# Output weights' squares moved from ScalarE to GpSimd, and the first norm's last step moved to ScalarE one set behind

## What is computed

```python
def _rfs(xw, ab, AB, gs):
    dot_products = jnp.einsum('...d,rd->...r', xw, ab[:, None] * gs)
    correction = (0.5 * jnp.sum(xw * xw, axis=-1))[..., None] * (ab * ab)
    return 1.0 / math.sqrt(NUM_RFS) * AB * jnp.exp(dot_products - correction)
weights = _rfs(input_weights, ab, AB, proj_matrix)
feats = _rfs(x, ab, AB, proj_matrix)
attn = jnp.einsum('bsr,or->bso', feats, weights)
x = _layernorm(x + attn)
gate, up = jnp.einsum('bsd,hd->bsh', x, wg), jnp.einsum('bsd,hd->bsh', x, wu)
x = _layernorm(x + jnp.einsum('bsh,dh->bsd', silu(gate) * up, wd))
```

## Time and profile before

| | |
|---|---|
| median of 3 runs | 609.4 us (609.28 to 609.42) |
| the profiled execution's own time | 610.9 us |
| its span on the slowest core (core 6) | 609.3 us; core 0 609.1, the 8 cores 605.9 to 609.3 us |
| TensorE busy | 590.8 us, 97% of the span |
| VectorE busy | 421.9 us, 69% |
| GpSimd busy | 381.9 us, 63% |
| ScalarE busy | 202.2 us, 33% |
| chain that ended last | TensorE 94%, transfers 3%, issue 1%, VectorE 1% |

### The profile page before, as it was taken

One profiled execution on the slowest core, in us unless ns is written; L12 is line 12 of the kernel. 1 busy time (PEld: TensorE's weight loads), 2 busy tenths in 40 slices (PEclk: granted clock), 3 DMA queues, 4 the chain that ended last, 5 costly groups with the idle time before them and its releaser, 6 DMA issues.

```text
span 609.3 us, 9120 instructions; the slowest of 8 cores (605.9 to 609.3 us)
## 1 busy us (share of the span) xinstructions
PE 590.8 (97%) x2649; PEld 266.1 (44%) x2703; DVE 421.9 (69%) x689; ACT 202.2 (33%) x375; POOL 381.9 (63%) x341
## 2 busy tenths in 40 slices
PE   5999999999999999999999999999999999999995
PEld 1444444444444444444444444444444444444442
DVE  2468323477788777777777777777777678876775
ACT  1234834447853322332232223222320015300243
POOL 9100899400093288999999999999516495604950
PEclk7988999999999999999999999999999999999999
DMA  8999471599930110422422413324424749983433
GB/s 143 155 169 235 154 234 34 169 279 324 232 85 2 69 40 32 164 93 73 165 86 80 165 47 118 116 84 158 146 104 126 254 147 306 318 266 136 175 138 140
DMA packets 45106, 90.79 MB, mean 149 GB/s; under 512 B 19328, under 2 KB 26496, under 8 KB 41728
## 3 DMA queue, kind: packets, MB, share of 16 engines
q1 hardware_dynamic: 36752, 59.52, 31.0%
q0 software_dynamic: 8160, 30.41, 19.3%
q10 hardware_dynamic: 144, 0.26, 0.1%
HBM read 60.82 MB, written 23.59 MB: 139 GB/s over the span
## 4 chain that ended last, share of the span: by engine, by line
PE 94%; DMA 3%; issue 1%; DVE 1%; POOL 0%; ACT 0%; DVEq 0%; ACTq 0%; POOLq 0%
PE P L597 47%; PE P L886 24%; PE P L321 9%; PE P L484 9%; PE P L366 5%; DMA proj<-projT 3%; PE P L399 1%; POOL xf L80 0%; POOL proj L80 0%; PE P L288 0%; PE P L290 0%; ACT junk L781 0%; DVE zh L829 0%; DVE wbuf L652 0%; DVE ebuf L616 0%
## 5 line engine op out<-in xcount | busy, mean ns | idle before, releaser
L597 PE MATMUL P<-x1t,ring 128*128 128x512 bf16 x753 | 180.1, 379 | 1.2 <-DVE ebuf L616 0.4
L210 POOL TENSOR_TENSOR ring<-ring 128x512 bf16<-128x512 bf16 x120 | 135.3, 1160 | 13.1 <-DMA ring<-wgu 9.6
L597 PE MATMUL P<-xsum,ring 128*128 128x512 bf16 x564 | 138.7, 379 | 0.6
L597 PEld LDWEIGHTS P<-x1t,ring 128*128 128x128 bf16 x768 | 75.0, 98 | 91.5 <-issue 1.6
L210 POOL TENSOR_TENSOR stage<-stage 128x512 bf16<-128x512 bf16 x60 | 68.1, 1170 | 46.1 <-DMA stage<-wd 44.2
L597 PEld LDWEIGHTS P<-xsum,ring 128*128 128x128 bf16 x576 | 56.4, 98 | 68.0 <-issue 0.4
L886 PE MATMUL P<-tbuf,hact 128*128 128x512 bf16 x376 | 83.3, 379 | 0.4
L321 PE MATMUL P<-xf,proj 128*128 128x512 bf16 x250 | 63.3, 413 | 6.0 <-ACT lnst L180 5.5
L886 PE MATMUL P<-tbuf,sbuf 128*128 128x512 bf16 x282 | 62.5, 379 | 0.3
L612 ACT ACTIVATE ebuf<-P 128x512 f32<-128x512 f32 x48 | 28.2, 588 | 101.4 <-PE P L597 101.4
L632 ACT ACTIVATE hact<-P 128x512 bf16<-128x512 f32 x48 | 28.5, 597 | 91.7 <-PE P L597 68.2
(11 more groups left out here) (94 smaller groups left out, 683.9 us busy)
## 6 DMA issues: line engine op xcount, KB each, us to landing
tbuf<-t_hbm SPq DMA_DIRECT2D x14, 1536.0 KB, 8.6
ring<-wgu POOLq DMA_DIRECT2D x12, 1024.0 KB, 5.3
xtok_sb<-xtok SPq DMA_DIRECT2D x16, 512.0 KB, 5.5
t_hbm<-stage SPq DMA_DIRECT2D x8, 896.0 KB, 4.4
stage<-wd POOLq DMA_DIRECT2D x12, 512.0 KB, 3.6
x_hbm<-x1k SPq DMA_DIRECT2D x16, 256.0 KB, 3.8
xres<-x_hbm SPq DMA_DIRECT2D x16, 256.0 KB, 6.5
out<-zd SPq DMA_DIRECT2D x8, 512.0 KB, 6.2
```

Source lines behind the costliest of these rows:

```text
L210: out[o] = (p.mark(eng, lambda e: e.tensor_tensor(d, a, b, op), *toks, *behind),)
L597: fn = lambda e, dk=dk, lhsT=lhsT, rhs=rhs: e.matmul(bank(b), lhsT, rhs, start=(start and dk == 0), stop=(stop and dk == 3), skip_group_ch ...
```

## The change

The squares of `norm_w` become GpSimd `tensor_tensor` multiplications. The place in the file is the same, but on GpSimd's queue they come behind the loads and ahead of all weight sums. All sets but the last have `apply` on ScalarE, with the shift as a 128x1 VectorE `tensor_tensor`, and the `apply` of a set is written behind the `root` of the next.

```diff
@@ norm_w
-        t_sq["w", k] = p.mark("scalar", lambda e: e.activation(sqw[:, a:b], iw[:, a:b], AF.Square), ld_iw[k])
+        t_sq["w", k] = p.mark("gpsimd", lambda e: e.tensor_tensor(
+            sqw[:, a:b], iw[:, a:b], iw[:, a:b], OP.mult), ld_iw[k])
@@
-    ON_ACT = range(7, NM - 1)
+    ON_ACT = range(NM - 1)
@@ apply
-                t_s = p.mark("scalar", lambda e: e.activation(shift, negm, AF.Copy, scale=rstd), t_r[0])
+                t_s = p.mark("vector", lambda e: e.tensor_tensor(shift, negm, rstd, OP.mult), t_r[0])
@@
         step = attn(i)
-        if 0 < i <= ON_ACT[0]:
-            last_norm[1]()
         if i < NM - 1:
             step[0]()
-        if i in ON_ACT:
-            step[1]()
+        if i > 0:
+            last_norm[1]()
```

## The result

The changed kernel takes **621.3 us** (median of 4 runs, 620.5 to 621.6) against 609.4 on the same chip: ratio 1.019, 95% interval 1.0178 to 1.0203, 11.9 us slower. The forecast was 624.0 in a range of 613 to 627. Its profiled execution took 620.5 us with a span of 619.0 on the slowest core, again core 6.

A forecast was written before the change was run, and what follows sets the result against it. TensorE, busy 97% of the span, was taken as the bound. For core 6, 11.0 + 1.7 + 1.25 + 0.6 = 14.6 us on the median 609.4 gave 624.0 us, range 613 to 627.

The forecast's parts named there:

- Turns of whole instructions: VectorE's five norm_x(3) instructions alternate with GpSimd's squares, each waiting for a whole instruction; they end at 73.5, not 56.7.
- The delay of 11.0: TensorE waits at feat_unit(3, 0) for banks whose evictions end at 76.7 but are wanted at 65.7: 11.0 us.
- The clock, 1.7: Work lost to a lower granted clock behind TensorE's long wait for banks: 1.7 us, bounds 0 and 3.4.
- Part 1: Squares leave ScalarE: core 0 loses its 2.0 us sbc wait and 1.7 us behind it; core 6 gains nothing.
- The seam, 1.25 + 0.6: At the first gate_up units: copy 1.25 us later behind set 14's shift, plus 0.6 for VectorE sums meeting GpSimd's.
- Part 3: apply on ScalarE, one set behind: nothing on TensorE's path, 10 us of matmuls ahead, except at the gate_up seam.
- A: Rival: VectorE's five norm_x(3) instructions are not held, or only by the first square; 610.7 us, chance 0.09.
- B: Rival: squares much faster than the sums, or only some of VectorE's five held; 613 to 619.5 us, chance 0.09.
- C: Rival, not slower: ScalarE's relief in w_unit(0) decides; 609.0 us, chance 0.05.

The follow-up runs named there:

- experiment 2: Kernel before with only the squares moved to GpSimd, in pieces of 1024 or 512 columns: 612.5 us (1.0055) and 611.7 us (1.003).
- norm_only: The changed kernel without the squares' move: squares stay on ScalarE, only the norm is changed; 611.75 us, ratio 1.0036.
- half_norm: Kernel before with the whole norm change, and the last two square quarters on GpSimd behind norm_x(3)'s last VectorE instruction: 609.7 us, ratio 1.0002.
- Experiment 4: norm_only with set 14's apply written right behind its own root: 611.6 us, ratio 1.004.
- sq_gated: Kernel before with the four squares on GpSimd, each waiting for the last VectorE instruction of norm_x(3); norm as before: 609.8 us, ratio 1.0015.
- sq_512: Kernel before with the squares on GpSimd in 16 pieces of 512 columns, norm as before: 611.7 us, ratio 1.003.

## Why the prediction was right

- **Turns of whole instructions (the basis of 11.0): right.** Four of the five are held on core 6, and the length of the hold follows the piece (experiment 2). The cores of the changed kernel's one execution say the same, since they differ in how many of the five began ahead of the first square: two held on core 1, and TensorE waits 3.0 us for `arg`; three on cores 2 and 4, 6.4; four on cores 0, 3, 6 and 7, 9.6; all five on core 5, the last of them in part, 10.1. Their spans go the same way: 612.7; 613.5 and 615.9; 617.1 to 619.0; 618.9. So the cores lie 6.3 us apart, not within 2 as forecast: how many are held hangs on when `iw` lands, and the slowest core sets the time.
- **The delay of 11.0: mis-sized, it is 9.6.** The five end at 68.5 where 73.5 was forecast, in the main for three reasons. The first L278 was not held (1.2 us). L283 waited for the fourth square and not for a weight sum behind it (1.2). And a square takes 3.59 us by itself and not 4.05 (1.8 for the four). The 4.04 to 4.58 with which the squares are recorded here hold VectorE's turns in them, so they do not confirm the 4.05. Against that, TensorE wants the banks at 60.2 and not at 65.05, since core 6 ran at full clock this time. The two errors, 5.0 and 4.9 us, cancel, and that is luck. What is left is the count of the evictions: the forecast set all four (3.2 us) ahead of TensorE, which in fact goes on bank by bank, 0.8 us behind the five's end, and then waits only 0.5 more.
- **The clock, 1.7: mis-sized, it is 3.0** on core 6. The low level lasts until about 75 us, some 6 us of work, where the earlier trace rows had 4. Counted the same way the eight cores lost 2.4 to 4.0 us, three of them more than the upper bound of 3.4. That 11.0 + 1.7 and 9.6 + 3.0 come to the same is luck too.
- **Part 1, "it gains nothing" on core 6: this is the step that left the sum 2.7 us too high.** In the profile of before the wait for `sbc` (1.6 to 2.0 us) stands on cores 0 to 3, and is missing on cores 4 to 7, whose granted clock was 0.81 to 0.84 over 50 to 65 us; cores 0 to 3 had 0.98 to 1.00. In `norm_only`, at 1.00, it stands on all eight. So the lower clock of that one execution hid the wait, and the change takes it away. `half_norm`, which is `norm_only` with two squares moved, has no such wait and is 2.0 us faster (609.7 against 611.75). Core 0's price was 3.7 us, with the clock behind it (2.0 and 1.7), and the 14.5 us of core 6 less 2.0 to 3.7 are 10.8 to 12.5, around the 11.9 measured. The forecast had the price and left it out, because it built its sum on one core of one execution. How much of it the slowest core of a median execution gets back is not shown; no trace of one was taken.
- **The seam, 1.25 + 0.6 = 1.85: the size is right (1.94), a mechanism partly wrong.** The copy is late behind the shift, as forecast: 0.99 + 0.19. The last two L210 did not meet GpSimd (0.68 us at 196.30). What did is set 15's `apply`, 2.22 us where before it took 1.30, and the one L210 that met it before too: 1.59, 1.40 then. Experiment 4 shows the same trade from the other side.
- **Part 3 off the path apart from the seam: right**: the norm's change costs 2.2 us by itself, and its waits are all at the seam, beside the one for `sbc` that was there before.
- **The rivals.** A (not held): refuted by the lengths; `sq_gated` is what it looks like, at 609.8. B (some not held) is what cores 1, 2 and 4 show; the slowest core decides. C, the relief of ScalarE: real, as part 1 shows, but smaller than the delay here, and without the delay given back at the first copy.
- On the Trainium skill (SBUF: State Buffer, Who interferes with whom): its lock for a whole instruction, on two-input work of both engines, is what the lengths of 3.90, 2.19 and 1.34 us show. Its sentence that issue order decides does not reach: here neither engine keeps its turn while the other waits. Its price for the square (GPSIMD Engine Reference, Elementwise: side-by-side cycle accounting), 4497 ns for fp32, is above the 3.59 us that bf16 takes undisturbed.

## What to carry to other kernels

Before work moves to GpSimd, lay its start beside what VectorE does then: each VectorE instruction with two SBUF inputs that met one here grew by nearly a whole GpSimd instruction, so the number of meetings times the length of one piece is the price to reckon with, and smaller pieces or a start behind VectorE's string took most of it or all of it away. Price a piece from a stretch where it meets nothing. Then ask what slack hides the delayed instructions, and what is queued behind them, and where TensorE will wait next if it comes earlier: here a transpose was late for it, and ScalarE's string, slower per set than TensorE, carried that to the seam. And build the sum on more than one core: a wait that the slowest core lacks in one profiled execution may be there on all of them in the next.

## What the runs showed of the hardware

- VectorE's and GpSimd's two-input instructions alternate when both have the next one ready, at every size tried (2048, 1024 and 512 columns); a held instruction is recorded as a long one.
- GpSimd's bf16 `tensor_tensor` of one operand with itself takes 3.59, 1.89 and 1.04 us at 2048, 1024 and 512 columns when it meets nothing.
- A `tensor_scalar` with one wide input is held too: 4.68 us for 0.81 of work, longer than the one 512-column sum (1.16) that a single turn would cost. It shows on four cores of `sq_512` (4.68 to 4.72), on each of which the `apply` starts 0.16 to 0.21 us behind the start of GpSimd's instruction that issues the 896 KB store of `t_hbm`. Why it takes so long is open.
- The granted clock was 0.50 from 65 us on, in waits of 9.1 us, on cores 0 and 6. Behind a wait of 2.0 us in `norm_only` the cores differ: 0.89 over 60 to 75 us on core 0, 1.00 on core 6.
- With TensorE busy without a gap, core 6 had 0.82 to 0.86 for 35 us in one execution (cores 4, 5 and 7 the same within 0.02, cores 0 to 3 0.93 and more), and 1.00 in another.
